# One load, two groups of row operations and three groups of weight splits moved in a two-layer transformer kernel

## The reference

```
h = layernorm(x) * (1 + ca) + sa          # ca, sa, ga, cb, sb, gb from a condition
x = x + ga * attention(h)
h = layernorm(x) * (1 + cb) + sb
x = x + gb * ffn(h)
```

## Time and profile before

| what | value |
| --- | --- |
| median of 3 runs | 2636.72 us (2635.99 to 2641.81) |
| the profiled execution's own time | 2641.81 us |
| its span | 2640.0 us |
| TensorE busy | 2412.7 us, 91% |
| VectorE busy | 1796.9 us, 68% |
| mean granted TensorE clock | 0.962 |

### The profile page before, as it was taken

One profiled execution on the slowest core, in us unless ns is written; L12 is line 12 of the kernel. 1 busy time (PEld: TensorE's weight loads), 2 busy tenths in 40 slices (PEclk: granted clock), 3 DMA queues, 4 the chain that ended last, 5 costly groups with the idle time before them and its releaser, 6 DMA issues. The chain is left out here.

```text
span 2640.0 us, 45233 instructions
## 1 busy us (share of the span) xinstructions
PE 2412.7 (91%) x16852; PEld 1983.4 (75%) x16852; DVE 1796.9 (68%) x3056; ACT 1348.8 (51%) x2031; POOL 927.3 (35%) x1046
## 2 busy tenths in 40 slices
PE   7999868999999999999999969999768888999998
PEld 5777655777777777777777758888657776888887
DVE  6888864886778767876777646666466657666664
ACT  5666533766666666665666733333234434332322
POOL 1233333464446354645444331212346641001000
PEclk8999988999999999999999979999879998999999
DMA  4011114433343334333433243332301104121221
GB/s 140 27 35 52 30 39 124 123 104 105 98 137 101 104 105 143 96 101 102 134 109 106 62 131 103 102 105 74 110 26 35 35 29 132 44 75 35 81 57 41
DMA packets 193802, 223.80 MB, mean 85 GB/s; under 512 B 37400, under 2 KB 157232, under 8 KB 189936
## 3 DMA queue, kind: packets, MB, share of 16 engines
q1 hardware_dynamic: 191792, 220.38, 28.3%
q10 hardware_dynamic: 1792, 0.53, 0.1%
HBM read 150.95 MB, written 55.73 MB: 78 GB/s over the span
## 5 line engine op out<-in xcount | busy, mean ns | idle before, releaser
L1240 DVE TENSOR_REDUCE l_negmax<-l_mx 128x1 f32<-128x512 f32 (+3 forms) x608 | 394.4, 654 | 131.7 <-PE l_mx L1637 130.5
L1486 ACT ACTIVATE l_Phi<-l_s 128x1024 fp32r<-128x1024 f32 x288 | 295.1, 1025 | 182.5 <-PE l_s L1659 176.0
L1252 DVE TENSOR_TENSOR l_Plo<-l_s,l_Phi 128x1024 fp32r<-128x1024 f32 x288 | 350.1, 1216 | 15.5 <-ACT l_s L1490 15.1
L1670 PE MATMUL l_o<-l_Phi,l_V 128*128 128x256 f32 x1152 | 307.0, 288 | 6.6 <-ACT l_Osb L1498 2.3
L1657 PE MATMUL l_s<-l_QA,l_KK 128*128 128x512 f32 x576 | 280.3, 487 | 27.2 <-DVE l_Plo L1252 23.5
L1670 PE MATMUL l_o<-l_Plo,l_V 128*128 128x256 f32 x1152 | 300.2, 282 | 0.0
L1490 ACT ACTIVATE l_s<-l_s 128x1024 f32<-128x1024 f32 x288 | 295.0, 1024 | 0.0
L2786 ACT ACTIVATE m_hidhi<-m_h 128x512 fp32r<-128x512 f32 x168 | 106.2, 632 | 359.5 <-DVE m_h L2635 359.5
L1637 PE MATMUL l_mx<-l_KK,l_QA 128*128 128x512 f32 (+3 forms) x768 | 271.7, 394 | 6.5 <-DVE l_negmax L1240 2.7
L1670 PEld LDWEIGHTS l_o<-l_Phi,l_V 128*128 128x128 f32 x1152 | 219.6, 191 | 40.4 <-issue 29.1
L1659 PE MATMUL l_s<-l_QB,l_KL 65*128 65x512 f32 x576 | 229.3, 398 | 0.0
(11 more groups left out here) (469 smaller groups left out, 6383.9 us busy)
## 6 DMA issues: line engine op xcount, KB each, us to landing
l_qd<-l_qs SPq DMA_DIRECT2D x256, 128.0 KB, 2.4
l_QA<-l_qd SPq DMA_DIRECT2D x64, 512.0 KB, 3.5
l_QB<-l_qd SPq DMA_DIRECT2D x64, 256.0 KB, 4.3
l_R<-l_rd SPq DMA_DIRECT2D x128, 128.0 KB, 2.9
m_spread<-m_combs SPq DMA_DIRECT2D x62, 256.0 KB, 5.1
m_spread<-m_combs SPq DMA_DIRECT2D x124, 128.0 KB, 4.9
xs<-next_store SPq DMA_DIRECT2D x32, 256.0 KB, 2.0
l_rps<-l_rp SPq DMA_DIRECT2D x128, 64.0 KB, 1.9
```

The lines of the kernel that those rows point to most:

```text
L1240: v.tensor_reduce(negmax[:, n % 2, at + h0:at + h1], piece_of(number, chunk), AX.X, ALU.max, negate=True).then_inc(reduced, 1)
L1252: v.tensor_tensor(Plo[:, s % 3].rearrange("p u h q -> p (u h q)"), S2[s % 2][:, :], Phi[:, s % 3].rearrange("p u h q -> p (u h q)").bitcas ...
L1486: a.activation(Phi[:, s % 3].rearrange("p u h q -> p (u h q)"), S2[s % 2][:, :], ACT.Exp, scale=L_D ** -0.5).then_inc(exped, 1)
L1670: mm = pe.matmul(O[:, odd * 2 * P:(odd + 1) * 2 * P].rearrange("p (j q) -> p j q", j=2), V[:, b % 2, k, 64 - 64 * odd:192 - 64 * odd], src ...
```

## The change

SyncE starts the load of the next sequence's rows two steps later. VectorE normalizes and divides two tiles in each of four units, (5, 5) to (5, 8) and (8, 4) to (8, 7), in place of one in each of eight. In rope attention the value weights' split stands ahead of all projections on VectorE. In `experts` GpSimd makes the low part of pieces 6 and 7 too, with a semaphore of their own (`split_last`); ScalarE's splits of 6, 7 and 8 stand ahead of the silu of jobs 0, 1 and 2; and in m1 `probabilities(0)` stands behind all six first splits.

```diff
@@ latent_attention, sync
-                if ahead and ls == 1:
+                if ahead and ls == 3:
                     load(b)
@@ latent_attention, vector
-                    at = UNITS * (ls - 5) + i - 3
-                    if 0 <= at < TT:
-                        normalize(b, at)
+                    if ls == 5 and i >= 5:
+                        normalize(b, 2 * i - 10)
+                        normalize(b, 2 * i - 9)
...
-                    at = UNITS * (ls - 8) + i - 3
-                    if 0 <= at < TT:
-                        rms(b, at)
+                    if ls == 8 and 4 <= i < 8:
+                        rms(b, 2 * i - 8)
+                        rms(b, 2 * i - 7)
@@ rope_attention, vector
-            split(0)
-            split(1)
+            for n in range(3):
+                split(n)
             for t in range(L.HEAD):
                 project(t)
-                if t == 5:
-                    split(2)
@@ experts, vector
-                if n in (NS + 1, NS + 2):
-                    split(5 + n - NS)
@@ experts, gpsimd
-                    .then_inc(split_down, 1)
+                    .then_inc(split_down if i % 3 == 2 else split_last, 1)
...
             for n in range(JOBS + 3):
+                if n == 0:
+                    split(6)
                 b, r = ahead(n)
                 if b is not None and r == 1:
                     inverse_root(b)
-                if n == NS + 2:
-                    split(8)
+                if n in (1, 2):
+                    split(6 + n)
@@ experts, scalar
             for i in range(6):
-                if i == 4 and not first:
-                    probabilities(0)
                 split(i)
...
-                if n == 0 and first:
+                if n == 0:
                     probabilities(0)
                 if n >= 1:
                     hidden_high(n - 1)
+                if n < 3:
+                    split(6 + n)
...
                     gate(n)
-                if n < 3:
-                    split(6 + n)
@@ experts, tensor
-                    if n < NT and j % PT_ == 0:
+                    if n < NT and j % PT_ == 0 and j < 2 * PT_:
                         pe.wait_ge(split_lo, 2 * (j // PT_) + which + 1)
+                    elif n < NT and j % PT_ == 0:
+                        pe.wait_ge(split_last, which + 1)
```

More of the change, by code:

```diff
@@ L2347, in experts @@
         shared_out = signal("shares")
+        split_last = signal("split_last")
         gate_done, up_done = signal("gate_done"), signal("up_done")
```

## The result

The changed kernel takes 2663.46 us, median of 4 executions (2661.84 to 2667.55), against 2636.35 (4 executions): a ratio of 1.0102, 95% interval 1.0086 to 1.0119, or 27.1 us more (22.7 to 31.4). The forecast was 14 us more, with a range that ended at 2662. The direction was right, the size was half, and the range missed by 1.5 us.

What follows compares the result with a forecast made beforehand. TensorE and VectorE were taken to run in step in latent attention with next to no slack. Terms 12.0 - 3.3 - 2.9 + 5.9 + 2.2 = +13.9 us gave 2650.6, called 2651, for a median; range 2641 to 2662.

Steps and rivals of the forecast that it cites:

- load: Latent attention: VectorE's first stats1 waits 4.9 us, TensorE shifts 3.0 in each of three places, plus 1.0 each for clock: +12.
- divisions in pairs: Latent attention, step 8: tiles are ready a unit earlier for the transposes, so TensorE's waits for L1214 go: -3.3 us.
- normalize in pairs: Latent attention, step 5: normalize ends earlier, but modulate on GpSimd starts at (5, 8) as before: 0.
- value split: Rope attention: the value projection no longer waits for VectorE's split, but for a bank emptied 2.1 us later: -2.9 us.
- experts: GpSimd's added splits stop VectorE's routing chain, and scores come late: +5.9 us in m1 and +2.2 in m0.
- The silu's own wait: Experts, m1: job 0's silu, queued behind piece 6, is ready at 2201.3, before VectorE's chain ends: costs nothing more.
- late scores: Experts, m1: scores come where the silu stood, so all of the routing chain runs after that point: +1.0 us.
- the two stalls: Experts, m1: GpSimd's splits of pieces 6 and 7 each stop VectorE's chain for their whole length: +2.45 us each.
- TensorE doesn't feel a late VectorE: Rival: score and maxima banks absorb the delay at stats1 and in experts, leaving only gains: -6.2 us, 2630.5; chance 0.08.
- Splits run beside the chain: Rival, experts: GpSimd's splits run beside VectorE's chain; m1 costs 1.0, m0 0: +6.8 us in all, 2643.5; chance 0.13.
- Other cause of the gap: Rival, rope attention: the 8.3 us gap isn't the split's, so the phase is 2.1 late: +18.9 us, 2655.6; chance 0.07.
- The clock falls harder: Rival: each of the load's three stops costs 6 us and m1 8: +22 us in all, 2658.7; chance 0.10.

Runs made afterwards that it cites:

- load3: The kernel before with only the load of the next sequence's rows two steps later: +12.9 us (8.7 to 17.2).
- rms2: The kernel before with only the divisions two tiles in a unit, (8, 4) to (8, 7): +7.9 us (5.0 to 10.8).
- norm2: The kernel before with only normalize two tiles in a unit, (5, 5) to (5, 8): +5.0 us (2.4 to 7.9).
- act_order: The kernel before with only ScalarE's new order in experts and the late scores; low parts of 6 and 7 stay on VectorE: -0.5 us (-3.2 to +2.1).
- value: The kernel before with only the value split of rope attention ahead of the projections: -2.4 us (-4.7 to -0.3).

## Why the prediction was right in direction and wrong in size

| part | forecast, us | alone, us |
| --- | --- | --- |
| load | +12.0 (9 to 15) | +12.9 (8.7 to 17.2) |
| divisions in pairs | -3.3 (-5 to 0) | +7.9 (5.0 to 10.8) |
| normalize in pairs | 0 | +5.0 (2.4 to 7.9), again +1.1 (-1.6 to 3.7) |
| value split | -2.9 (-3.4 to +2) | -2.4 (-4.7 to -0.3) |
| experts | +8.1 (1 to 13) | +6.6 (3.4 to 9.5) |
| sum | +13.9 | 26 to 30; the whole change 27.1 |

The load, both kinds of pairs and the experts were measured in one job, and of these only `normalize` was measured again, with a smaller result. So the single terms are known to some 3 us each, the load's to 4.

- **The load**: right in arrival, VectorE's wait and the shift of TensorE, which fell on the row maxima and not on the scores. In `load3` TensorE's waits for row maxima grow by 9.1 us (2.7 to 11.8), where 9.0 were forecast. The clock falls as forecast; that it costs 1 us in each place is not measured by itself.
- **The divisions**: the step that failed. The first half was right: TensorE's 3.3 us for L1214 went. The second half, that "two in a row can delay one low part by about as much", priced the added row by its undisturbed length. Two units lie between two low parts, so two pairs do: 1.2 us of VectorE's time undisturbed, and 3.6 (1.99 and 1.63 in the trace of `rms2`) under GpSimd's L1390 and L1396. In the kernel before two single rows stood there, 1.9 us, and no row met L1396. TensorE then waits 2.4 us, and its clock falls. Less the 1.1 us that goes, each place costs some 1.3 us of waiting and the low clock behind it; the eight matmuls of L1585 take 3.62, 2.28 and 3.04 us in the three places of `rms2`, where they took 1.89 before. Three times 1.3, and the 3.3 us that these matmuls lose, make an estimate of 7.2, beside the 7.9 measured. The trace of before held the warning, VectorE's rows and then GpSimd's:

```profile
581.29 1.08 DVE L1214 TENSOR_SCALAR next_rows<-next_store,next_rstd 128x256 f32<-128x256 f32 x1
...
582.89 0.83 DVE L1214 TENSOR_SCALAR next_rows<-next_store,next_rstd 128x256 f32<-128x256 f32 x1
...
585.96 0.34 DVE L1214 TENSOR_SCALAR next_rows<-next_store,next_rstd 128x256 f32<-128x256 f32 x1
```

```profile
580.95 2.62 POOL L1390 TENSOR_TENSOR l_Osb<-l_Osb,l_R 64x512 f32<-64x512 f32 x2 [2.33 <-DMA l_R<-l_rd]
584.53 1.29 POOL L1396 TENSOR_TENSOR l_Ylo<-l_Osb,l_Yhi 128x512 fp32r<-128x512 f32 x1 [0.96 <-ACT l_Yhi L1504]
```

Under L1390 a row takes 1.08 and 0.83 us, clear of it 0.34. I looked for GpSimd's rows in the experts and not here. The term is 11.2 of the 13.2 us that the forecast lacked. What is left is the balance of the others, among them normalize, whose size is not settled.
- **Normalize**: put at nothing because `modulate` starts where it did. GpSimd's rows on the pairs were not looked at here either; they take up to 2.12 us (`norm2`) where 0.73 is the undisturbed length.
- **The value split**: right, with what is late next named rightly (`r_hThi`).
- **The experts**: 6.6 for 8.1. In the trace of after, m0 grows by 2.1 us from its first weight split on (forecast 2.2), m1 by 4.6 until job 1 (forecast 5.9), of which by the end of the trace m1 is only 2.0 longer; kernels with the experts unchanged differ by as much and more over m1 (451.6 to 457.7 us), so it is not shown that the rest comes back. The silu's own wait, which the prediction called free, makes the up products of job 1 0.55 us later than `m_h` alone would. The terms of m1 one by one: late scores 0.8 in the trace of `act_order`, as the later `m_h` of job 0 against the block's start (forecast 1.0), and the two stalls 2.25 - 0.22 = 2.0 and 4.35 - 2.29 = 2.1 (forecast 2.45 each). The prediction's other value for m1, 3.5 if the large comparisons were not stopped, is refuted by the second of them.
- **The rivals**: "TensorE doesn't feel a late VectorE" is refuted by the earlier trace rows and by `load3`. "Splits run beside the chain" is refuted by the rows of 2.25 and 4.35 us. "Other cause of the gap" is refuted by `value`. "The clock falls harder", 22 us, was nearest to the result and for the wrong place: the clock behind the load was as forecast, and fell at the divisions, where no term had put a wait.

The same section of the Trainium skill that the prediction used for the splits ("SBUF — State Buffer", "Who interferes with whom") also says that a `tensor_scalar` in VectorE's two-port mode takes the pair shared with GpSimd, and that the later of the two is blocked for a whole instruction. The trace agrees in the stop: one tile takes 0.34 alone and 1.08 under L1390; in which mode the row runs no trace here shows. By that sentence the divisions had to be laid beside GpSimd's rows before they were priced.

## What to carry to other kernels

Before work is moved or bunched on VectorE, lay GpSimd's rows of the same microseconds beside it: the price of a row is what it takes there, and the place in the kernel before where the same row is two or three times its usual length shows what is coming. Where two engines run in step, count what falls between two of the rows that TensorE waits for, and not what is added in a unit. A load can be late for nothing up to the row that needs it (step 2, 0 us), and a step more costs most of its lateness (16.1 us of waiting on VectorE, 12.9 us of time in `load3`), in each of the three places.

## What the runs showed of the hardware

- Two VectorE rows of L1214 in a row under two GpSimd rows don't wait once, but once for each: 0.60 for the pair alone, 1.75 and 1.99 under L1390. Singly, with a row maximum between, they took 1.08 and 0.83, so the two waits under L1390 are about the same (1.2 us together, against 1.15 and 1.39). What the pairs add is the next pair in front of the same low part, and its wait of 1.0 us under L1396.
- It goes the other way, too. GpSimd's split of 1024 columns takes 2.39 us beside short rows of VectorE and 4.14 beside ranks of 2048 columns, the VectorE row of 2.29 then 4.35: both lose, one behind the other. The split ends 2.25 us behind the end of one rank (2226.25 against 2224.00), and the next rank 2.14 behind the end of the split (2228.39).
- Around and behind waits of 2.4 to 2.9 us on TensorE the granted clock of windows of three and four microseconds was 0.50 (`rms2`), 0.58 and 0.67 (after); 0.50 is the lower of its levels, 1.2 GHz, for the whole window. Around the wait of 1.13 us for L1214 in step 8 of the kernel before it stayed at 1.00 (windows from 580 to 592).
